# Middle attention of a graph network kernel: the attention product in two halves of query columns, scores three items ahead, value projection between the first scores

## The reference

```
routing = x.mean(axis=1);  sel = argmax(relu(routing @ r_w1 + r_b1) @ r_w2 + r_b2)
q, k, v = x @ wq[sel], x @ wk[sel], x @ wv[sel]          # 625 x 512, as 8 heads of 64
scores  = einsum('bhqd,bhkd->bhqk', q, k) / sqrt(64)
attn    = softmax(scores, axis=-1)                       # 8 heads x 625 x 625
out     = einsum('bhqk,bhkd->bhqd', attn, v) -> 625 x 512;   x = x + out @ wo[sel]
```

## Time and profile before

| | us |
|---|---|
| median of 3 runs | 2615.51 |
| lowest, highest | 2601.01, 2616.03 |
| the profiled execution, its own time | 2604.54 |
| its span on the core | 2602.7 |
| PE busy | 2427.9 |
| DVE, POOL, ACT busy | 1808.2, 1660.4, 935.5 |
| first matmul of the value projection | at 396.71 |
| first score | at 412.29 |
| first attention product | at 429.74 |
| last attention product | at 524.41 |
| first matmul of the output projection | at 532.39 |

### The profile page before, as it was taken

The page is one execution under the profiler, slowest core; times in us unless marked ns, Lnnn a source line. Parts: engine busy times, 40 slices in busy tenths (PEclk is TensorE's granted clock), DMA queues, the critical chain, the costliest instruction groups (busy, mean ns, idle before and its releaser), DMA issues.

```text
span 2602.7 us, 34427 instructions
## 1 busy us (share of the span) xinstructions
PE 2427.9 (93%) x11600; PEld 2028.2 (78%) x11600; DVE 1808.2 (69%) x2651; ACT 935.5 (36%) x1144; POOL 1660.4 (64%) x724
## 2 busy tenths in 40 slices
PE   6989978886899569999999999999999999999999
PEld 6878877775899567777777777777777777777777
DVE  8984336656698557777777777777777777777775
ACT  3732226522498542222232222322223222223221
POOL 0034323248888646777777777777777777777773
PEclk9999879986899779999999999999999999999999
DMA  3024010021433211122221222212122121221211
GB/s 77 16 76 155 17 65 17 1 74 40 114 91 82 66 38 65 65 97 78 83 97 64 97 75 86 97 64 97 73 88 97 64 97 71 90 97 64 97 65 36
DMA packets 49889, 190.90 MB, mean 73 GB/s; under 512 B 13300, under 2 KB 17911, under 8 KB 33444
## 3 DMA queue, kind: packets, MB, share of 16 engines
q1 hardware_dynamic: 35728, 177.90, 19.6%
q0 software_dynamic: 13200, 10.75, 1.9%
q10 hardware_dynamic: 900, 1.44, 0.2%
HBM read 177.54 MB, written 12.35 MB: 73 GB/s over the span
## 4 chain that ended last, share of the span: by engine, by line
PE 83%; DVE 9%; POOL 4%; issue 2%; ACT 2%; DMA 1%; SPq 0%; DVEq 0%; ACTq 0%; POOLq 0%
PE PS L1719 25%; PE PS L1721 25%; PE PS L1720 24%; PE PS L1983 2%; PE PS L1984 2%; POOL gatW L757 2%; PE PS L1797 2%; DVE hotS L1165 1%; DVE hotD L1166 1%; POOL XN L757 1%; DVE negmax L1412 1%; PE PS L1734 0%; DVE XN L1129 0%; DVE PTl L1426 0%; POOL Wl L693 0%
## 5 line engine op out<-in xcount | busy, mean ns | idle before, releaser
L1669 DVE SCALAR_TENSOR_TENSOR XN<-PS,attn,XN 125x512 f32<-125x512 f32 x1083 | 805.3, 748 | 441.6 <-PE PS L1721 432.9
L795 POOL TENSOR_TENSOR OPl<-TS,OPh 128x1024 fp32r<-128x1024 f32 x256 | 676.7, 2644 | 117.6 <-ACT OPh L1075 117.6
L795 POOL TENSOR_TENSOR OPl<-RAW,OPh 128x1024 fp32r<-128x1024 f32 x192 | 555.0, 2890 | 274.8 <-ACT OPh L1075 274.7
L1719 PE MATMUL PS<-OPh,XTh 128*125 128x512 f32 x1280 | 507.4, 396 | 2.0 <-DVE attn L1623 2.0
L1721 PE MATMUL PS<-OPh,XTl 128*125 128x512 f32 x1280 | 506.1, 395 | 0.0
L1720 PE MATMUL PS<-OPl,XTh 128*125 128x512 f32 x1280 | 503.6, 393 | 0.0
L1075 ACT ACTIVATE OPh<-TS 128x1024 fp32r<-128x1024 f32 x256 | 271.8, 1062 | 529.3 <-PE PS L1721 519.3
L1075 ACT ACTIVATE OPh<-RAW 128x1024 fp32r<-128x1024 f32 x192 | 203.9, 1062 | 581.0 <-PE PS L1721 581.0
L1719 PE MATMUL PS<-OPh,Sh 128*125 128x512 f32 x1024 | 404.7, 395 | 3.4 <-DVE XN L1666 3.4
L1721 PE MATMUL PS<-OPh,Sl 128*125 128x512 f32 x1024 | 404.1, 395 | 0.0
L1720 PE MATMUL PS<-OPl,Sh 128*125 128x512 f32 x1024 | 402.7, 393 | 0.0
(11 more groups left out here) (349 smaller groups left out, 3529.2 us busy)
## 6 DMA issues: line engine op xcount, KB each, us to landing
RAW<-in_values SPq DMA_DIRECT2D x64, 2048.0 KB, 7.5
filters<-filt SPq DMA_DIRECT2D x14, 672.0 KB
fil<-filters SPq DMA_DIRECT2D x11, 840.0 KB
Wraw<-in_ffn SPq DMA_DIRECT2D x4, 1024.0 KB, 5.3
Wraw<-in_L_q SPq DMA_DIRECT2D x2, 1024.0 KB, 5.1
Wraw<-in_L_k SPq DMA_DIRECT2D x2, 1024.0 KB, 8.4
Wraw<-in_L_v SPq DMA_DIRECT2D x2, 1024.0 KB, 7.3
gatW<-nodes,dstI POOLq DMA_INDIRECT x90, 3.6
```

The costliest lines, as they stand in the source:

```text
L795: g.tensor_tensor(OPl[:, j], operand_source(j, parity), OPh[:, j].bitcast(F32), ALU.subtract).then_inc(op_lower, 1)
L1669: v.scalar_tensor_tensor(out=XN[:, t], in0=PS[0:P, bank, :], scalar=w, in1=XN[:, t], op0=ALU.mult, op1=ALU.add).then_inc(v_added, 1)
L1719: mm(dst, lh, rh, start=start, stop=False, skip_group_check=resumed)
```

## The change

It touches the attention stage only.
- The product of a head is two units of 15 matmuls, one for each half of the query columns. The first needs the transposed probabilities of tiles 0 to 2 and is issued after the fourth tile's probT; the second needs all five and is issued after the first probT of the next head. Each uses one bank of its slot and has a drain of its own, of 314 columns.
- LAG is 3: score i stands with probT i-3. No steps are merged. Five steps of a head read, in letters: S P A, S P, S P, S P A, S P.
- The three value units stand ahead of scores 0, 1 and 2, on every engine.
- In DVE's loop the drain of a probT comes ahead of that of an attn of the same step.
- The split of L1_q comes after the last item, on ACT and on POOL.
- PE waits for the keys of a head pair as it comes to it, and for the padding of `PTh` ahead of the first product.

```diff
-LAG = 2
+LAG = 3
...
+def attention_step(i):
+    turned = i - LAG
+    parts = []
+    if i < len(TILES):
+        parts.append(("v1", i))
+    if i < ITEMS:
+        parts.append(("score", i))
+    if 0 <= turned < ITEMS:
+        parts.append(("probT", turned))
+    if turned > 0 and turned % T == T - 2:
+        parts.append(("attn", turned // T * 2))
+    if turned > 0 and turned % T == 0:
+        parts.append(("attn", turned // T * 2 - 1))
+    return parts
+
+ATTENTION = [part for i in range(ATTENTION_STEPS) for part in attention_step(i)]
...
                 if part == "attn":
-                    head = n
-                    u, c = ("attn", head), slice(head // 2 * 128, head // 2 * 128 + 128)
+                    head, h = n // 2, n % 2
+                    u, c, queries = ("attn", n), slice(...), slice(h * HN, (h + 1) * HN)
                     begin(u)
-                    wait_drained(pe, ("probT", T * head + T - 1))
-                    for h in range(2):
-                        queries = slice(h * HN, (h + 1) * HN)
-                        for t in range(T):
-                            ins = product(slot(u)[:, h, 0:HN], ...)
+                    if n == 0:
+                        pe.wait_ge(pt_padded, 1)
+                    wait_drained(pe, ("probT", T * head + (T - 1 if h else 2)))
+                    for t in range(T):
+                        ins = product(slot(u)[:, 0, 0:HN], ...)
                     finish(ins)
...
+                for part, n in attention_step(i - 1) if i else ():      # DVE, iteration i, after max(i) and reciprocal(i-1)
+                    u = (part, n)
+                    if part == "v1":      rest(u, VFl[:, j], ...)
+                    if part == "attn":    rest(u, halves(XTl[...])[:, h], slot(u)[o:o + 64, 0, 0:HN], ...)
+                    if part == "probT":   ... PTl[:, 0:4, c] ...; rest(u, PTl[:, 4, c], ...)
```

More of the change, by code:

```diff
@@ L76 @@
 UNITS += [(s + "0", i) for s, i in CONTEXT_AND_ROWS]
-LAG = 2
-UNITS += [("mean", 0), ("hidden", 0), ("logits", 0)] + [(s, i) for s, n in (("xt1", T), ("q1", K), ("k1", K), ("v1", 3)) for i in range(n)]
+LAG = 3
+UNITS += [("mean", 0), ("hidden", 0), ("logits", 0)] + [(s, i) for s, n in (("xt1", T), ("q1", K), ("k1", K)) for i in range(n)]
 ITEMS = HEADS * T
[L83 to L98, removed]
+ATTENTION_STEPS = ITEMS + LAG + 1
+def attention_step(i):
[13 more added lines that the diff above has]
+ATTENTION = [part for i in range(ATTENTION_STEPS) for part in attention_step(i)]
 UNITS += ATTENTION
@@ L733, in _ @@
             split_weight(WEIGHT["F_o"])
-            split_weight(WEIGHT["L1_q"])
             for i in range(ITEMS):
@@ L739, in _ @@
                                 ALU.mult, ALU.mult).then_inc(prob_ready, 1)
+            split_weight(WEIGHT["L1_q"])
             pool.wait_ge(in_loaded, 16)
@@ L968, in _ @@
             weight_upper(WEIGHT["F_o"])
[L969 to L973, removed]
             for part, n in ATTENTION:
@@ L982, in _ @@
                                  accum_out=rowsum[:, item:item + 1]).then_inc(drained_s, 1)
+                if part == "v1":
+                    u, tiles = ("v1", n), TILES[n]
+                    wait_filled(u)
+                    upper(u, VFh[:, tiles[0]:tiles[-1] + 1], slot(u)[0:P, 0:len(tiles), :])
                 if part == "attn":
-                    head = n
-                    u, o = ("attn", head), 64 * (head % 2)
+                    head, h = n // 2, n % 2
+                    u, o = ("attn", n), 64 * (head % 2)
                     wait_filled(u)
-                    upper(u, halves(XTh[o:o + 64, head // 2]), slot(u)[o:o + 64, :, 0:HN])
+                    upper(u, halves(XTh[o:o + 64, head // 2])[:, h], slot(u)[o:o + 64, 0, 0:HN])
                 if part == "probT":
@@ L993, in _ @@
                     upper(u, PTh[:, 4, c], slot(u)[0:P, 1, 0:P])
+            weight_upper(WEIGHT["L1_q"])
             layer_std(2)
@@ L1402, in _ @@
                 ins.then_inc(drained_v, 1)
-            for m, tiles in enumerate(TILES):
-                u, j = ("v1", m), slice(tiles[0], tiles[-1] + 1)
-                rest(u, VFl[:, j], slot(u)[0:P, 0:len(tiles), :], VFh[:, j])
             v.memset(PTh[:, :, N:NT].bitcast(F32), 0.0)
             v.memset(PTl[:, :, N:NT].bitcast(F32), 0.0).then_inc(pt_padded, 1)
-            for i in range(ITEMS + LAG + 2):
+            for i in range(ATTENTION_STEPS + 1):
                 if i < ITEMS:
@@ L1417, in _ @@
                     v.reciprocal(rinv[:, n:n + 1], rowsum[:, n:n + 1]).then_inc(rinv_ready, 1)
[L1419 to L1428, removed]
+                for part, n in attention_step(i - 1) if i else ():
+                    u = (part, n)
+                    if part == "v1":
+                        j = slice(TILES[n][0], TILES[n][-1] + 1)
+                        rest(u, VFl[:, j], slot(u)[0:P, 0:len(TILES[n]), :], VFh[:, j])
+                    if part == "attn":
+                        head, h = n // 2, n % 2
+                        o = 64 * (head % 2)
+                        rest(u, halves(XTl[o:o + 64, head // 2])[:, h], slot(u)[o:o + 64, 0, 0:HN], halves(XTh[o:o + 64, head // 2])[:, h])
+                    if part == "probT":
+                        c = tile_columns(n % T)
+                        dve.wait_ge(upper_ready, splits(u))
+                        v.tensor_tensor(PTl[:, 0:4, c], slot(u)[0:P, 0, 0:4 * P].rearrange("p (k n) -> p k n", k=4),
+                                        PTh[:, 0:4, c].bitcast(F32), ALU.subtract)
+                        rest(u, PTl[:, 4, c], slot(u)[0:P, 1, 0:P], PTh[:, 4, c])
             for m, tiles in enumerate(TILES):
@@ L1907, in _ @@
             node_columns("k1", WEIGHT["F_k"])
-            node_rows("v1", WEIGHT["F_v"])
-            pe.wait_ge(pt_padded, 1)
             for part, n in ATTENTION:
@@ L1914, in _ @@
                     begin(u)
-                    if item == 0:
-                        wait_drained(pe, ("k1", K - 1))
+                    if item % (2 * T) == 0:
+                        wait_drained(pe, ("k1", head // 2))
                     c = tile_columns(item % T)
@@ L1942, in _ @@
                     finish(ins)
-            wait_drained(pe, ("attn", HEADS - 1))
+            wait_drained(pe, ("attn", 2 * HEADS - 1))
             node_rows("proj1", WEIGHT["F_o"])
```

9 lines of the change are left out of this document (6 added, 3 removed).

## The result

The changed kernel takes **2631.17 us** (median of 6 runs, 2624.88 to 2633.27) against 2608.82 for the kernel before beside it (6 runs, 2597.36 to 2617.36): a ratio of 1.0081, 95% interval 1.0058 to 1.0104. Forecast were 2625 us and a change of less than 1%. The profiled execution took 2631.75 us, with a span of 2629.9. One execution of a later kernel (both orders with the first half later), at 2678.44 us and a mean granted clock of 0.867 against 0.954 to 0.957 in its other three, is left out of that kernel's ratio.

What follows compares the result with a forecast made beforehand. PE's waits for probT drains behind DVE's next maximum were taken to bound the attention stage; start -4.0, distances +18.7, end +0.3 give +15 us, so 2619.5 by profile or 2630.5 by median, 2625 taken between; range 2602 to 2656.

Steps and rivals of the forecast that it cites:

- The cycle: One head of the attention stage: five waits of PE for drains make it 16.4 us against 13.5.
- Se to Sa: Within a head's cycle: the fifth step's score to the next head's first, which waits for a probT slot, 2.56 us.
- the 1.85 and 1.70: Intervals in us behind DVE's maximum: 1.85 until a product can start, 1.70 until a slot is free for PE's score.
- The seven distances: Attention stage, first to last head's first product half: 113.4 us instead of 94.7, +18.7.
- The start: Value units between the first scores: first product half at 425.7, 4.0 us earlier, despite waits for slots.
- The end: Last head's chain to the output projection, at 547.1 against 532.39; this part adds +0.3 us.
- The sum: Whole kernel: start -4.0, distances +18.7, end +0.3, together +15 us.
- rival 1: Attention stage: new pauses make PE's clock fall, 2668 us if wholly slow, 2644 at half of that; 19%.
- signs that the forecast had named for being wrong: In the attention stage: cycles under 13.5 us, or clock rows of 0.50 amid the stage.
- Rival 2: Attention stage: product halves fill the gaps at the five waits and PE bounds, -33 us, 2571; 9%.
- Rival 3: Attention stage: the five waits are each 0.3 us shorter, cycle 14.9, +6, or 2610 us; 10%.
- Rival 4: Stage start: it gives nothing, the third value unit and three scores waiting longer for slots, +19; within the forecast's range (62%).

Runs made afterwards that it cites:

- both orders with the first half later: Changed kernel with ACT's rounding ahead of the exponential, DVE's rest ahead of the maximum, and the product's first half issued one step later: ratio 0.9905 to the kernel before.
- values first: Changed kernel with its three value units made and drained ahead of the first score again: 2633.17 us profiled, stage 155.61.
- DVE's order alone: Changed kernel with DVE taking the rest of the last step's probT ahead of the new maximum, ACT's order unchanged: 2640.71 us profiled, stage 165.22.
- whole product: Changed kernel with a head's product undivided again, 30 matmuls in one unit: 2624.9 us profiled, stage 151.82.
- lead of two: Changed kernel with scores two items ahead instead of three: 2636.8 us profiled, stage 162.54.
- ACT's order alone: Changed kernel with ACT rounding the probT ahead of the step's exponential, DVE's order unchanged: 2627.5 us profiled, stage 154.79.
- first half later: Changed kernel with the first half of a product issued one step later, drain orders unchanged: 2605.9 us profiled, stage 136.48.
- early drains, whole product: Changed kernel with ACT and DVE taking product and probT drains ahead of exponential and maximum, product undivided: 2619.14 us profiled, stage 138.52.
- short maximum: Changed kernel with the row maximum over the first 156 of 625 columns, order untouched: 2611.32 us profiled, stage 137.45.
- early drains, lead of two: Changed kernel with both drain orders turned, first half one step later, scores two ahead, value rests ahead of the maximum: 2590.87 us profiled, stage 122.21.
- both orders: Changed kernel with ACT rounding the probT before the exponential and DVE taking its rest before the next maximum: 2599.45 us profiled, stage 124.39.
- both, first half later, with and without values first: Changed kernel, both drain orders turned, first half one step later; with value units ahead of the first score: 2589.14 us, ratio 0.9908; without: ratio 0.9905.

## Why the prediction was right

**The cycle: right, by its own steps.** Forecast Se to Sa 2.56, Sa to A1 2.56, A1 to Sb 2.22, Sb to Sc 2.56, Sc to Sd 1.21, Sd to P3 1.35, P3 to A0 1.71, A0 to Se 2.22: 16.39. The rows above give 2.48, 2.80, 2.23, 2.49, 1.15, 1.56, 1.64 and 2.25: 16.60. Only Sa to A1 is off by more than 0.21 us: a product starts later behind its maximum than a score does, as the 1.85 and 1.70 of the forecast already had it, and there it took the score's. The waits read shorter in the rows than in the sum (5.4 in all instead of 6.05) at least in part because a matmul's row is 0.31 long where the next could have started 0.15 after it.

**The seven distances: +21.6 instead of +18.7.** They came to 116.3 us: 16.45, 16.60, 16.40, 18.95, 16.46, 16.62 and 14.82. The forecast's own steps give 113.1 for the seven (4.8 + 6 x 16.4 + 9.9), not the 113.4 of its sum, so +18.4, and 3.2 us are missing. The fourth distance is the mis-sized term. It has 6.8 us at half clock and is 2.4 longer than its neighbours, with waits that are no longer than theirs (4.9 us in all against 5.2 to 5.4). The other 0.8 us is spread over the other six.

**The start: -2.9 instead of -4.0.** v(2) waited 2.22 us (forecast 2.3), and S3 and S4 waited as summed:

```profile
421.91 0.63 PE L1726 MATMUL PS<-Wh,XTh 128*125 128x512 f32 x1 [2.22 <-DVE VFl L1143]
...
429.18 0.41 PE L1925 MATMUL PS<-keys_high,queries_both 128*125 128x314 f32 x1 [2.09 <-DVE VFl L1143]
```

Behind the first of these waits the granted clock was 0.62 for 4.5 us (the stretch 421.90 to 426.40 above). The 12 matmuls of the unit took 4.45 us, until S2 at 426.36, where 0.2325 each makes 2.79: 1.66 lost. v(2) had begun 0.14 us sooner than summed, and from S2 to the first product it took 11.06 instead of 11.4, so 1.2 of it are left, the missing 1.1. The sum was right in its waits, but it did not ask what the start would be without the interleaving: "values first" shows a gain of 7.1 us there.

**The end: +1.8 instead of +0.3.** From the last A0 to the output projection 9.78 us instead of 7.98. The 14 distances between the matmuls of the last half product took 3.63 us (558.52 to 562.15), 0.26 each over most of them, where 0.146 each makes 2.05: +1.6, which is the whole miss (clock 0.83 over the stretch). The L1_q split behind the items cost nothing that shows: what follows the stage took 2066.4 us against 2070.3, within the 2060.5 to 2072.4 of all runs.

**The sum**: -2.9 + 21.6 + 1.8 = +20.5, against the stage's +20.6 and the forecast's +15 (14.7 by its steps). The medians differ by 22.35. The three places with half clock make 2.4 + 1.7 + 1.6 = 5.7 us of the 5.9 in excess; what else was off nearly cancels. So **rival 1** was right in kind and came at about a tenth of its full price. One of the signs that the forecast had named for being wrong was there: the granted clock was 0.51 from 493.60 to 500.50, amid the stage, not 1.00. Over the whole stage 13.7 us were at half clock against 10.2 before, and of the seven cycles one had any. The Trainium skill, page "TensorE: Matmul & The Clock Gate", section "A second HAM failure mode: psum-queue depth-cycling", has the clock swing where brief idles separate groups of matmuls. The traces agree in part: with DVE's order alone at least 3.4 us of every head were at half clock, with the changed order 6.8 us in one cycle of seven and none in the rest.

**Rival 2** (the halves fill the gaps) was put at 9%, and the ground against it was "one S to its drain is 2.56 us, and no order of DVE's list changes that". Of DVE's list alone the one order tried gave no shorter cycle. But the ground left out ACT's list: with both turned the cycle is 12.5, and 11.9 with the first half later, nearer to the 10.5 of PE's issue. The forecast of this kernel did not need that sentence, the judgement of the idea did. **Rival 3** (shorter waits) was not seen: no distance between products that has a full head's scores was 14.9. Rival 4 fell with the first product's 2.9 us.

The range held the time, but it is 54 us wide and would have held a change of nothing as well; what bears the account out is the cycle with its five waits in their places. What carried it was writing the unit four places earlier behind each unit, and then asking where that unit's drain stands in DVE's list.

## What to carry to other kernels

A wait for a buffer is a wait for everything that stands ahead of its drain on the draining engine, so before a unit is split or moved on the matmul engine, write for each wait what the drain stands behind there. If two engines drain one after the other, look at both lists together: here one alone gave 1.5 us with the cycle unchanged and the other a loss of 9.0, which went with 28 us more at half clock, and both gave 31.9. A half, a lead or a split is worth only what the drains let through: the same halves cost 1.5 us a head with late drains and gave 1.7 with early ones, against the one whole product tried there.

## What the runs showed of the hardware

The granted clock fell in heads whose longest pause of PE was 1.3 to 2.45 us, though not in all of them, and in no full head with shorter ones. For each kernel, the longest pauses in a head, the sum of all, and the distances between one head's first product and the next's that have half-clock time in them; the last distance is apart, since other pauses stand in it:

| kernel | longest pauses, us | all, us | of six | the last |
|---|---|---|---|---|
| DVE's order alone | 2.45 and 1.15 to 1.30 | 4.4 to 4.8 | six | yes |
| whole product | 1.87 to 1.89 and 1.12 to 1.27 | 3.6 to 3.7 | four | yes |
| lead of two | 1.29 to 1.42, 1.20, 1.20 | 5.0 to 5.4 | three | yes |
| values first | the same | 4.9 to 5.4 | two | no |
| changed, ACT's order alone | the same | 4.9 to 5.4 | one each | no |
| first half later | 1.29 to 1.32 and 1.2 to 1.29 | 3.3 to 3.5 | none | no |
| early drains, whole product | 1.04 to 1.20 and 0.8 | 2.9 to 3.1 | none | no |
| short maximum | 0.89 to 0.93 and 0.8 | 3.2 to 3.4 | none | no |
| before | 0.91 and 0.87 | 2.2 | none | yes |
| early drains, lead of two | 0.82 to 0.86, three times | 2.4 | none | yes |
| both orders | 0.45 to 0.61 | 1.1 to 1.5 | none | no |
| both, first half later, with and without values first | 0.37 to 0.48 | 0.8 to 1.1 | none | no |

A fall took 1.5 us (3.4 us at half clock) or 2.4 to 2.5 us (6.8) from a cycle. What decides between two heads with equal pauses the runs don't show, and it stays open.

Half-clock time also goes with the spread from run to run: over 14 profiles with the same instructions ahead of the stage, it was 68.3 to 92.2 us there, and the stage began at 396.71 with the least of it, at 400.1 to 404.7 in the six with 71.7 to 75.1 us, and at 404.7 to 410.3 in the seven with more.

Drains of half a product (64 rows of 314 columns) took 0.43 us on ACT and 0.46 to 0.49 on DVE, against 0.69 and 0.81 for the whole one: two halves cost 0.1 to 0.2 us more on each.
